# Mean and variance of the fourth norm made by ScalarE with accumulated sums instead of by VectorE

## The reference, cut to what matters

```python
h = _layernorm(x) * (1 + ca) + sa;  x = x + ga * dilated_attention(h)      # norm 1
h = _layernorm(x) * (1 + cb) + sb;  x = x + gb * quantised_ffn(h)          # norm 2
h = _layernorm(x) * (1 + ca) + sa;  x = x + ga * mamba(h)                  # norm 3
h = _layernorm(x) * (1 + cb) + sb;  x = x + gb * recurrent_gates(h)        # norm 4

def _layernorm(x, axis=-1, eps=1e-05):
    m = jnp.mean(x, axis=axis, keepdims=True)
    v = jnp.var(x, axis=axis, keepdims=True)
    return (x - m) / jnp.sqrt(v + eps)
```

## Time and profile before

| what | before |
|---|---|
| time, median of 3 runs | 1268.17 us (1267.76 to 1268.23) |
| profiled execution, span of its instructions | 1264.5 us |
| granted TensorE clock, mean of the span | 0.986 |
| HBM traffic | 248 GB/s over the span |

### The profile page before, as it was taken

The page is one execution under the profiler, slowest core; times in us unless marked ns, Lnnn a source line. Parts: engine busy times, 40 slices in busy tenths (PEclk is TensorE's granted clock), DMA queues, the critical chain, the costliest instruction groups (busy, mean ns, idle before and its releaser), DMA issues.

```text
span 1264.5 us, 12574 instructions
## 1 busy us (share of the span) xinstructions
PE 1140.8 (90%) x3612; PEld 640.1 (51%) x3612; DVE 1155.2 (91%) x1138; ACT 795.0 (63%) x1445; POOL 982.6 (78%) x712
## 2 busy tenths in 40 slices
PE   7989678998999899997999899997999899789996
PEld 5636333664457444764457443763457443444453
DVE  3768999999999999899999999899999999999987
ACT  2256567765786668755786668755786667655532
POOL 3216886889778887989778997889778996976862
PEclk9999989999999999999999999999999999899998
DMA  7308588766868688866878679876868786899922
GB/s 285 115 16 315 176 269 284 278 233 233 281 226 297 200 278 292 289 233 225 290 219 301 197 277 311 276 241 217 292 217 287 215 282 236 290 335 346 374 86 116
DMA packets 92309, 313.87 MB, mean 248 GB/s; under 512 B 10432, under 2 KB 15680, under 8 KB 91984
## 3 DMA queue, kind: packets, MB, share of 16 engines
q1 hardware_dynamic: 89936, 306.26, 70.3%
q10 hardware_dynamic: 2304, 6.82, 1.5%
HBM read 301.73 MB, written 11.31 MB: 248 GB/s over the span
## 4 chain that ended last, share of the span: by engine, by line
PE 43%; DVE 22%; POOL 14%; ACT 9%; issue 8%; DMA 3%; SPq 0%; DVEq 0%; POOLq 0%; ACTq 0%
PE ps L907 13%; DVE ps L1741 12%; POOL arena L1970 8%; PE ps L601 5%; PE ps L830 4%; PE ps L609 3%; DVE arena L1749 3%; DMA arena<-bc_scratch 2%; PE ps L647 2%; PE ps L751 2%; PE ps L723 2%; ACT ps L1295 2%; ACT arena L931 2%; PE ps L728 1%; PE ps L633 1%
## 5 line engine op out<-in xcount | busy, mean ns | idle before, releaser
L1970 POOL TENSOR_TENSOR arena<-arena 128x1024 f32<-128x1024 f32 x255 | 600.3, 2362 | 136.5 <-PE ps L907 113.2
L1741 DVE TENSOR_TENSOR_SCAN ps<-ps,arena 128x1024 f32<-128x1024 f32 (+1 forms) x257 | 585.8, 2280 | 30.3 <-ACT ps L1295 17.9
L907 PE MATMUL ps<-arena,identF 128*128 128x512 f32 x1024 | 482.8, 603 | 49.0 <-DVE arena L1749 29.4
L1295 ACT ACTIVATE ps<-arena,negA 128x512 f32<-128x512 f32 x512 | 332.7, 683 | 83.2 <-DVE arena L1749 78.2
L907 PEld LDWEIGHTS ps<-arena,identF 128*128 128x128 f32 x1024 | 190.3, 193 | 267.2 <-issue 208.8
L1749 DVE TENSOR_TENSOR arena<-ps,arena 128x1024 f32<-128x1024 f32 (+1 forms) x257 | 312.0, 1214 | 5.9
L922 ACT ACTIVATE arena<-arena,rnln 128x256 f32<-128x256 f32 x118 | 61.9, 589 | 42.1 <-POOL rnln L1776 24.9
L647 PE MATMUL ps<-arena,inw 128*128 128x512 f32 x128 | 60.0, 614 | 11.7 <-ACT arena L931 9.6
L1307 ACT ACTIVATE arena<-ps 128x2 f32<-128x2 f32 x128 | 22.0, 172 | 64.9 <-DVE arena L1749 64.4
L931 ACT ACTIVATE arena<-ps,modT 128x512 f32<-128x512 f32 x43 | 51.7, 1266 | 14.7 <-PE ps L474 12.6
L728 PE MATMUL ps<-arena,inw 128*128 128x512 f32 x128 | 60.2, 592 | 0.0
(11 more groups left out here) (222 smaller groups left out, 1707.1 us busy)
## 6 DMA issues: line engine op xcount, KB each, us to landing
arena<-bc_scratch SPq DMA_DIRECT2D x511, 512.0 KB, 5.0
arena<-in_x SPq DMA_DIRECT2D x16, 256.0 KB, 6.9
arena<-in_x SPq DMA_DIRECT2D x8, 512.0 KB, 8.4
xr_scratch<-arena SPq DMA_DIRECT2D x6, 512.0 KB, 6.9
px_scratch<-arena SPq DMA_DIRECT2D x6, 512.0 KB, 6.1
out_x<-arena SPq DMA_DIRECT2D x5, 512.0 KB, 2.6
arena<-bc_scratch SPq DMA_DIRECT2D x9, 256.0 KB, 3.6
woT<-in_woT SPq DMA_DIRECT2D x4, 512.0 KB, 10.0
```

The source lines that it names most:

```text
L907: x = pe.matmul(ps[:, Y, :], identF[:], inp[:, m % RING, q, :], start=False, stop=(i == BLOCK_STEPS - 1 and q == 1), skip_group_check=True)
L1295: x = act.activation(ps[:, 2 * (m % 2) + q, :], dt[:, kd, :], ACT.Exp, scale=negA[:, kd, 2 * i + q:2 * i + q + 1])
L1741: x = dve.tensor_tensor_scan(states, states, inp[:, m % RING, q, :].rearrange("p q t -> p (q t)"), 0.0, ALU.mult, ALU.add)
L1970: x = pool.tensor_tensor(inp[:, m % RING, :, :], u[:, kd:kd + 1, :].broadcast_to([P, 2, TH]), b_at[:, m % 3, :, :], ALU.mult)
```

## The change

The statistics of norm 4 for halves 0 to 6 move from VectorE to ScalarE. VectorE's four bn_stats and four bn_aggr go. ScalarE gets four passes of Identity with an accumulated sum (row sums, due 6.25 and 6.5), and, once GpSimd has made the negated mean, four passes of Square with that mean as bias and an accumulated sum (due 7.25 and 7.5). Each pass also writes its full result into `hnA`, which is overwritten later. GpSimd's four small operations become one (`pool_mean`, due 6.75) and three (`pool_spread`, due 7.75). The rows of hnA move from 8 and 8.5 to 9 and 9.25 and stand in a chain of their own.

```diff
-            "px": (26.75, 28), "hnA": (8, 8.5)},
+            "px": (26.75, 28), "hnA": (9, 9.25)},
+    "act_after": {"ln4_sq": (7.25, 7.5), "ln4_sum": (6.25, 6.5), ...
-    "dve_after": {"ln4_stats": 6.25, "z": (6.5, 7.75, 8.25, 9.75), "ln4_moments": 6.5},
+    "dve_after": {"z": (6.5, 7.75, 8.25, 9.75)},
-    "pool_after": {"cp_gate": -7.25, "cp_add": (5, 5), "ln4_rstd": 6.75, ...
+    "pool_after": {"ln4_mean": 6.75, "cp_gate": -7.25, "cp_add": (5, 5), "ln4_rstd": 7.75, ...
+        def act_row_sums(site, spare, src, j):
+            mv = norm[site][1]
+            for jj in (j, j + 1):
+                x = act.activation(spare[:, jj, :], src[:, jj, :], ACT.Identity, accum_out=mv[:, jj, 0:1])
+            if j:
+                x.then_inc(ln[site].stats, 1)
+
+        def act_row_squares(site, spare, src, h, j):
+            mv, vn = norm[site][1:3]
+            act.wait_ge(ln[site].step, 3 * h + 1)
+            for jj in (j, j + 1):
+                x = act.activation(spare[:, jj, :], src[:, jj, :], ACT.Square, bias=vn[:, 1, jj:jj + 1], accum_out=mv[:, jj, 1:2])
+            if j:
+                x.then_inc(ln[site].aggr, 1)
+        def act_last_norm(g):
+            t, T = after(g), TIMES["act_after"]
+            for j in (0, 2):
+                yield t + T["ln4_sum"][j // 2]
+                act.wait_ge(S.resA, 2 * g + 2)
+                if g:
+                    act.wait_ge(S.px_out, 16 * g)
+                act_row_sums("ln4", hnA, xrows[g % 3], j)
+            for j in (0, 2):
+                yield t + T["ln4_sq"][j // 2]
+                act_row_squares("ln4", hnA, xrows[g % 3], g, j)
+            for j in (0, 2):
+                yield t + T["hnA"][j // 2]
+                act.wait_ge(ln["ln4"].nb, g + 1)
+                act_ln_rows("ln4", hnA, xrows[g % 3], g, j)
+        def pool_mean(site, h):
+            pool.wait_ge(L.stats, h + 1)
+            pool.tensor_scalar(vn[:, 1, :], mv[:, :, 0], -1.0 / E, None, ALU.mult).then_inc(L.step, 1)
+        def pool_spread(site, h):
+            pool.wait_ge(L.aggr, h + 1)
+            pool.tensor_scalar(vn[:, 0, :], mv[:, :, 1], 1.0 / E, EPS, ALU.mult, ALU.add).then_inc(L.step, 1)
+            pool.wait_ge(L.step, 3 * h + 2)
+            pool.tensor_tensor(rn[:, 0, :], vn[:, 0, :], neghalf, ALU.pow).then_inc(L.step, 1)
+            pool.wait_ge(L.step, 3 * h + 3)
+            pool.tensor_tensor(rn[:, 1, :], rn[:, 0, :], vn[:, 1, :], ALU.mult).then_inc(L.nb, 1)
```

More of the change, by code:

```diff
@@ L66 @@
         "softplus": (33.75, 33.75), "dt_copy": 41.25, "xc_silu": 28.5},
-    "act_after": {"cp_ev": (2.75, 5), "z_tanh": (5.75, 8, 8.5, 9.25), "hA": (10.25, 10.25),
+    "act_after": {"ln4_sq": (7.25, 7.5), "ln4_sum": (6.25, 6.5), "cp_ev": (2.75, 5), "z_tanh": (5.75, 8, 8.5, 9.25), "hA": (10.25, 10.25),
         "gate": (12.25, 15.75, 17.5, 20.25, 22.5, 26), "sigmoid": (11.5, 17.5, 17, 21.5, 22.5, 25.25),
-        "px": (26.75, 28), "hnA": (8, 8.5)},
+        "px": (26.75, 28), "hnA": (9, 9.25)},
     "dve_before": {"ln1_stats": -4.5, "ln1_moments": -4, "smax": (2.5, 6.5), "rsum": (6.5, 8.75), "ln2_stats": 13.25,
@@ L82 @@
         "ln3_rstd": 22.75, "u": (34.5, 39.25), "cut": (34.5, 42)},
-    "pool_after": {"cp_gate": -7.25, "cp_add": (5, 5), "ln4_rstd": 6.75, "f_c": 21, "i_g": 25.5, "c_new": 25.5},
+    "pool_after": {"ln4_mean": 6.75, "cp_gate": -7.25, "cp_add": (5, 5), "ln4_rstd": 7.75, "f_c": 21, "i_g": 25.5, "c_new": 25.5},
 }
@@ L1175, in act_after @@
                 act.activation(sz[:, kd, :], ps[:, z_bank(g + 1, kd), :], ACT.Tanh, scale=0.5).then_inc(S.z_tanh, 1)
[L1176 to L1182, removed]
             if g < 0:
@@ L1321, in act_program @@
             chains = [act_first()] + [act_after(g) for g in range(-1, G - 1)] + [act_before(h) for h in range(1, G)]
+            chains += [act_last_norm(g) for g in range(G - 1)]
             chains += [act_last()]
@@ L1622, in dve_after @@
             t = after(g)
[L1623 to L1627, removed]
             for kd in range(KD):
@@ L1630, in dve_after @@
                 dve_z(g + 1, kd)
-                if kd == 0 and g >= 0:
-                    yield t + TIMES["dve_after"]["ln4_moments"]
-                    dve_moments("ln4", g)
         def dve_final():
@@ L1764, in pool_rstd @@
             pool.wait_ge(L.step, 3 * h + 1)
+            pool.tensor_tensor(rn[:, 0, :], vn[:, 0, :], neghalf, ALU.pow).then_inc(L.step, 1)
+            pool.wait_ge(L.step, 3 * h + 3)
+            pool.tensor_tensor(rn[:, 1, :], rn[:, 0, :], vn[:, 1, :], ALU.mult).then_inc(L.nb, 1)
+        def pool_mean(site, h):
+            L = ln[site]
+            mv, vn = norm[site][1:3]
+            pool.wait_ge(L.stats, h + 1)
+            pool.tensor_scalar(vn[:, 1, :], mv[:, :, 0], -1.0 / E, None, ALU.mult).then_inc(L.step, 1)
+        def pool_spread(site, h):
+            L = ln[site]
+            mv, vn, rn = norm[site][1:]
+            pool.wait_ge(L.aggr, h + 1)
+            pool.tensor_scalar(vn[:, 0, :], mv[:, :, 1], 1.0 / E, EPS, ALU.mult, ALU.add).then_inc(L.step, 1)
+            pool.wait_ge(L.step, 3 * h + 2)
             pool.tensor_tensor(rn[:, 0, :], vn[:, 0, :], neghalf, ALU.pow).then_inc(L.step, 1)
@@ L1918, in pool_after @@
                 pool_add_branch(xrows[g % 3], tmpA, q, S.cp_tmp, S.resA, 2 * g + q + 1)
+            yield t + TIMES["pool_after"]["ln4_mean"]
+            pool_mean("ln4", g)
             yield t + TIMES["pool_after"]["ln4_rstd"]
-            pool_rstd("ln4", g)
+            pool_spread("ln4", g)
             yield t + TIMES["pool_after"]["f_c"]
```

## The result

The changed kernel takes 1281.35 us (median of 4 runs, 1280.21 to 1282.01) against 1268.2 us (1267.76 to 1269.17, 4 runs). The ratio is 1.0104, 95% interval 1.009 to 1.0118: about 13 us slower, where 6.8 were forecast. Its profiled execution spans 1278.9 us at a mean granted clock of 0.978; before it was 1264.5 us at 0.986, 14.4 us less.

What follows compares the result with a forecast made beforehand. VectorE was taken not to be the bound in six of seven windows, where ScalarE, GpSimd and TensorE lead. 3 x 1.3 (even) + 3 x 1.5 (odd) - 1.6 (window 6) = 6.8 us on 1268.17: 1275.0 us, range 1266 to 1284.

Steps and rivals of the forecast that it cites:

- the likeliest case: Delays on ScalarE and GpSimd outweigh VectorE's saving: 1275.0 us, own range 1273 to 1281, chance 0.69.
- VectorE's eight instructions are worth nothing in windows 0 to 5: There z 0 still waits for ScalarE's z_tanh 0, so VectorE's freed time, about 1.6 us a norm, becomes waiting.
- ScalarE's passes, 0.34 and 0.47 us: Pitch of one Identity and one Square pass with accumulated sum; four of each make 3.24 us a norm.
- z_tanh 1 late by 1.2 and 1.7 us: ScalarE's passes stand ahead of z_tanh 1; less hidden idle time it is 1.2 us late in even, 1.7 in odd windows.
- Even windows +1.3: GpSimd's moved norm 4 operations, 1.46 us, stand ahead of input 10; GpSimd starts norm 2 0.15 us earlier: 1.3 us late.
- Odd windows +1.5: hn2 0.5 us late plus 1.0 us of hnA rows ahead of decay 10 delay D copy, TensorE and input 14 by 1.5 us.
- After the window nothing takes the delay back: Behind q_scale every engine waits for a late one, so the program goes on shifted as a whole.
- hnA "adds nothing": hnA is needed only for TensorE's transposes at step 10.25, behind the D copy, so its own lateness adds nothing.
- Signs: Profile signs: z 1 waits over 2 us, z 0 about 1.7, q_scale near 1.4; half period about 144.4 us.
- A: Rival: VectorE is the bound after all, each of seven norms gives 1.6 us: 11.3 us less, 1256.9; chance 0.13.
- B: Rival: it cancels, cheaper passes, moved GpSimd operations half hidden in waits, hnA off the chain: 0.8 us, 1269; chance 0.11.
- C: Rival: Square is not in ScalarE's loaded table, so loads of 1.283 us are added: 23 us, 1291; chance 0.07.

Runs made afterwards that it cites:

- e7: Kernel before with VectorE's eight norm 4 statistics instructions replaced by one memset for halves 0 to 6, nothing added on ScalarE: 1265.74 us, 0.9973.
- e3: Changed kernel with unread repeat matmuls keeping TensorE busy ahead of the D copy (z 3 twice; in window 6 z 0 three times): 1275.2 us, 1.0052.
- e5: Kernel before with only the rows of hnA moved from 8 and 8.5 to 9 and 9.25: 1276.76 us, 1.0066.
- e2: Kernel before with ScalarE's eight passes added, sums to a spare tile, nothing moved, statistics still on VectorE: 1272.85 us, 1.0032.
- e6: Kernel before with z 3's matmuls run twice and, in window 6, z 0's twice more, results unread: 1268.85 us, 0.9994.
- e4: Kernel before with the change made in window 6 alone, no repeated matmuls: 1266.82 us, 0.9983.
- e1: Kernel before with the order alone: GpSimd's four norm 4 operations moved to 7.75, hnA to 9 and 9.25, statistics still on VectorE: 1282.05 us, 1.0105.

## Why the prediction came out as it did

Direction and range held: slower, 1281.35 inside 1266 to 1284, though 0.35 us above the likeliest case's own range. The size was 6 us short, 6.8 for 13. That the range held is in part luck: its upper end stood there for a dearer accumulator read or one more microsecond a window, and what filled it was the clock. The bound of 12.8 us, for an accumulator read of 0.216 us, agrees with the measured 13 by accident, since that read costs 0.09. Step by step:

*VectorE's eight instructions are worth nothing in windows 0 to 5.* Right, and shown by e7: 0.0 us in each. In window 6 they are worth 1.56 us at step 7, forecast 1.6.

*ScalarE's passes, 0.34 and 0.47 us.* A little low: 561.19 - 560.79 = 0.40 and 565.06 - 564.57 = 0.49 us, 3.56 us a norm for 3.24. From the start of a pass to its accumulator read it is 0.31 and 0.40 us, from there to the next pass 0.09 us both times: that is the accumulator read, as I had taken it from the earlier trace rows. Its own row lasts 0.19 us, of which half lies under the next pass. The Trainium skill, "ScalarE: Activation LUTs", section "What ACT_TABLE_LOAD costs", gives 0.31 and 0.40 us for them without the sum (worked out from its figures), and the trace agrees. The Identity's 0.06 us lie in the 0.24 us that I took off the 0.49 us of 512 numbers for 256 fewer: the pass without its sum is 0.31 us, only 0.18 less.

*z_tanh 1 late by 1.2 and 1.7 us.* Measured, as VectorE's longer wait for it: 2.16 - 0.54 = 1.6 in window 2, 2.57 - 0.54 = 2.0 in window 3. VectorE reaches z 1 about 0.3 us sooner without the bn_aggr, so the delay is 1.3 and 1.7 us (z_tanh 1 itself starts 566.54 - 560.84 - 4.32 = 1.38 us late in window 2). Right.

*Even windows +1.3.* It is 1.64. Norm 2's first operation on GpSimd starts at 569.69 - 4.32 = 565.37, as before, so the 0.15 us that I let input 9 win do not come: it waits 0.90 us for TensorE. Norm 2's four operations take 0.12 us longer (1.90 for 1.78), and norm 4's three take 573.11 - 571.59 = 1.52 us. Together 1.64, to the hundredth what the scans show. The mechanism was right, and the term was read 0.3 us too small.

*Odd windows +1.5.* The chain is as described. Window 3 after, the wait of z 1, the start of norm 2 on GpSimd, the six rows and the D copy on ScalarE:

```profile
713.45 0.69 DVE L1489 SCALAR_TENSOR_TENSOR arena<-arena,ps 128x512 f32<-128x512 f32 x1 [2.57 <-ACT arena L1192]
...
715.96 0.23 POOL L1781 TENSOR_SCALAR vnln<-mvln 128x4 f32<-128x4 f32 x1 [0.73 <-DVE mvln L1365]
...
717.80 3.06 ACT L922 ACTIVATE arena<-arena,rnln 128x256 f32<-128x256 f32 x6 [0.99 <-POOL rnln L1786]
...
722.19 0.67 ACT L1344 ACTIVATE ps<-arena,vecs 128x512 f32<-128x512 f32 x1
```

The D copy before, in window 3:

```profile
714.21 0.67 ACT L1318 ACTIVATE ps<-arena,vecs 128x512 f32<-128x512 f32 x1
```

With the 6.38 us built up before it, the D copy is 722.19 - 714.21 - 6.38 = 1.60 us late, forecast 1.5, and GpSimd has the 0.73 us wait for VectorE's aggregate that the forecast had as 0.5 us of delay. e3's odd windows add another 0.36 us at steps 23 to 25, outside the window. "After the window nothing takes the delay back" was right; that something adds to it there was not seen. In the profile after, window 1 has a 0.63 us wait of VectorE for a row transfer at step 23, which the kernel before has not; e3's 0.36 us are something else: in its windows 1 and 3 the four operations of VectorE between steps 23 and 24 take 2.87 and 2.90 us for 2.72, and its wait for TensorE behind step 25 is 0.70 us for 0.53. Why they are longer is open.

*hnA "adds nothing" beyond the 1.0 us; even windows hide it behind GpSimd's 1.3.* Right in size, 0.4 and 1.0 us in e5.

*Signs.* z 0's wait (1.69 us), z 1's wait of over 2 us in windows 0 to 5 and the missing wait ahead of norm 2's statistics came as named. VectorE's wait for q_scale is 0.98 us and not near 1.4; its busy time fell by 9.8 us for 12, ScalarE's rose by 23.2 for 25 to 30, and the period of a half grew from 143.3 to 145.6 us, clock losses included, for 144.4.

*What failed: the sum had no term for TensorE's clock.* The forecast put the D copy 1.0 to 1.5 us later and stopped at GpSimd's input 14. But TensorE's idle time ahead of the D copy, 1.88 us in window 2, was there in the trace before, and the change lengthens it to 2.18. What lengthens it is hnA: moved alone it makes it 2.86 us (e5), while the passes alone shorten it to 1.23 (e2, window 2), perhaps because TensorE's z matmuls come later too (not traced). In the profile after, four windows pay for a lower clock, 5.4 us in all, and window 6, forecast to gain 1.6, ends at +2.0. There the wait was 2.85 us before; the hnA rows make it 3.56 us (e5, hnA alone, has the same 3.56; e2, the passes alone, the old 2.85), the six sums take 5.46 us and VectorE loses 2.72 us. The last 0.7 us come from the stretch at step 26. By the medians, e3 takes 1281.35 - 1275.2 = 6.2 us off (6.6 by the two ratios, as the series differ). In the traces, order and passes are 9.6 us against the 6.8 forecast, and the difference is 3 x 0.34 + 3 x 0.5 + 0.3. By its ratio e3 is 6.6 us (5.0 to 8.1) slower than before, which looks like the forecast; but the median execution of before has some 2.4 us more than the profiled one, so this agreement is in part luck.

*Rivals.* A (VectorE the bound) is dead by e7. B's overlap of moved operations with waits does not happen in even windows, where they cost 1.5 us; in odd ones they cost 0.6, but hnA's 1.0 and the passes' 1.3 us are there on the chain. C is dead too: the loads stay at x13 on this line and at 33 in all, and Square runs among Tanh, Exp and Copy without one, though the Trainium skill, "ScalarE: Activation LUTs", section "Table sets: the hidden batching unit", doesn't name it among the functions that stand in every set.

*Around the span.* I took 1268.17 - 1264.5 = 3.7 us as time outside the span. For most executions it isn't: they take 1.3 us more than they span (1280.21 and 1278.9 for after, 1269.01 and 1267.7 for e6), a few of before up to 2.5 and one of e4 3.5. With 1.3 us, the median of before would span 1266.9 us, 2.4 more than the profiled execution, and 53 other executions of before in three series span 1265.6 to 1270.7: the profiled one was shorter than all of them. It did no harm to the forecast, since a difference was added to a median; the traces' differences of span to before are larger than those of the ratios in all twelve kernels, by 0.5 to 4.0 us. e3, e5, e6 and e7, for example, are 1.0 to 2.0 us behind that trace before window 0 begins.

## What to carry to other kernels

Taking work off the busiest engine was worth nothing here where that engine had a wait behind the work; look for the place where it has none (here window 6) and change that alone. A moved instruction can cost more than itself, by what it then stands in front of: here moving four rows and four tiny operations cost as much as the whole change. Before adding delay, look at TensorE's idle times: waits of 2 to 3 us in a full stretch were where a delay was paid twice here, and matmuls that nobody reads, put into the wait, were cheaper than the lower clock.

## What was unexpected in the hardware

- Six sums after a TensorE idle time took 2.81 us after 1.88 us (before), 2.86 us (e5, window 2) and 2.85 us (e1, window 0), but 4.51 us after 2.18, 2.33 and 2.78 us. Within one execution of the changed kernel, 2.18 us gave 4.51 in window 2 and 2.81 in window 4; and 3.56 us gave 5.46 (after) and 2.81 (e4). On the chain such a stretch cost between 0.2 us (e1, window 2) and 2.7 us. The kernel before, which has such waits too, measured from 1266.9 to 1272.1 us in three series; that the clock makes this spread is likely and not shown. The Trainium skill, "TensorE: Matmul & The Clock Gate", section "Part 1: The HAM clock gate (the "warmup" mystery)", calls the number of matmuls at the lower level at a kernel's start run-variable; these rows show the same later in a kernel.
- An accumulated sum on ScalarE adds about 0.09 us to the pitch of 256-number passes, while its own row reads 0.19 us.
- Every kernel without the statistics on VectorE in window 6 ended 0.9 us sooner behind the last scan, and every one with them did not. All of it lies behind the issue of the last two output transfers, which landed in 2.7 us (median) instead of 3.4. The cause wasn't tried.
